# Expert windows that finish their own rows: a residual add and a scatter in each window, sorting in two steps, separate waits for high and low halves, and two whole weight parts instead of three

## The reference

```python
def _L0_ffn_ref(x, w_gate, b_gate, W1, b1, W2, b2):
    logits = x_flat @ w_gate + b_gate
    probs = jax.nn.softmax(logits, axis=-1)
    route_p = jnp.max(probs, axis=-1)
    route_idx = jnp.argmax(probs, axis=-1)
    h = jax.nn.relu(jnp.einsum('nd,edm->enm', x_flat, W1) + b1[:, None, :])
    y = jnp.einsum('enm,emd->end', h, W2) + b2[:, None, :]
    return (y[route_idx, jnp.arange(n)] * route_p[:, None]).reshape(b, t, d)
x = x + _L0_ffn_ref(_layernorm(x, axis=-1), ...)
```

## Time and profile before

| | us |
|---|---|
| time, median of 3 runs | 441.27 (439.25 to 441.68) |
| the profiled execution's own time | 440.8 |
| its span, first to last instruction | 439.1 |
| first matmul of the first window | 187.2 |
| last product of the last window done | 421.2 |
| TensorE busy | 402.3 (92%) |
| VectorE busy | 319.6 (73%) |
| ScalarE busy | 257.0 (59%) |
| GpSimd busy | 34.9 (8%) |

### The profile page before, as it was taken

The page is one execution under the profiler, slowest core; times in us unless marked ns, Lnnn a source line. Parts: engine busy times, 40 slices in busy tenths (PEclk is TensorE's granted clock), DMA queues, the critical chain, the costliest instruction groups (busy, mean ns, idle before and its releaser), DMA issues.

```text
span 439.1 us, 5615 instructions
## 1 busy us (share of the span) xinstructions
PE 402.3 (92%) x1660; PEld 280.6 (64%) x1660; DVE 319.6 (73%) x497; ACT 257.0 (59%) x388; POOL 34.9 (8%) x41
## 2 busy tenths in 40 slices
PE   5999999999999897799998999999999999999930
PEld 2855576577874356577775777767777776767710
DVE  2768767798441886579797597979889797988802
ACT  4779687773000021377686667968686796867600
POOL 2100000000000010000200202001020201002022
PEclk9799899999999997989999999999999999999995
DMA  8995382695519800100069998699898989600005
GB/s 244 414 424 184 137 294 90 223 347 195 193 48 405 312 1 6 37 15 0 0 215 355 357 406 320 199 383 368 324 355 346 351 327 373 231 1 25 1 24 191
DMA packets 33695, 95.72 MB, mean 218 GB/s; under 512 B 2690, under 2 KB 3330, under 8 KB 32132
## 3 DMA queue, kind: packets, MB, share of 16 engines
q1 hardware_dynamic: 30900, 91.61, 56.4%
q0 software_dynamic: 1136, 3.67, 2.4%
q10 hardware_dynamic: 1632, 0.11, 0.3%
HBM read 91.72 MB, written 3.67 MB: 217 GB/s over the span
## 4 chain that ended last, share of the span: by engine, by line
PE 64%; DVE 19%; issue 7%; ACT 4%; DMA 3%; POOL 1%; DVEq 0%; SPq 0%; POOLq 0%; ACTq 0%
PE bank L1463 29%; DVE w_lo L1135 12%; PE bank L1298 6%; PE bank L1279 5%; PE bank L1308 3%; DVE h_lo L1130 3%; PE bank L1232 2%; DMA ring<-in_wq_t 2%; DVE work L1122 2%; PE bank L1478 2%; PE bank L1344 2%; PE bank L1320 2%; PE bank L1287 2%; ACT ring L522 1%; PE bank L1224 1%
## 5 line engine op out<-in xcount | busy, mean ns | idle before, releaser
L1135 DVE TENSOR_TENSOR w_lo<-ring,w_hi 128x1024 fp32r<-128x1024 f32 x117 | 145.3, 1267 | 33.8 <-ACT w_hi L688 32.8
L688 ACT ACTIVATE w_hi<-ring 128x1024 fp32r<-128x1024 f32 x117 | 122.3, 1054 | 54.0 <-PE bank L1463 53.0
L1463 PE MATMUL bank<-w_hi,x_hi 128*128 128x512 f32 x144 | 49.2, 423 | 5.6 <-DVE x_lo L1149 3.2
L1463 PE MATMUL bank<-ring,work 128*128 128x512 f32 x108 | 49.9, 598 | 0.3
L1463 PE MATMUL bank<-w_hi,x_lo 128*128 128x512 f32 x144 | 45.2, 395 | 0.0
L1463 PE MATMUL bank<-w_lo,x_hi 128*128 128x512 f32 x144 | 44.9, 393 | 0.0
L1463 PEld LDWEIGHTS bank<-w_hi,x_hi 128*128 128x128 f32 x144 | 26.5, 190 | 14.6 <-issue 8.5
L1463 PE MATMUL bank<-w_hi,h_hi 128*128 128x512 f32 x90 | 33.4, 452 | 1.5 <-DVE h_lo L1130 1.5
L1203 POOL TENSOR_TENSOR small<-small,work 128x512 f32<-128x512 f32 x9 | 16.0, 1775 | 231.1 <-ACT small L694 231.1
L1463 PEld LDWEIGHTS bank<-ring,work 128*128 128x128 f32 x108 | 19.7, 189 | 20.1 <-issue 19.4
L1463 PEld LDWEIGHTS bank<-w_hi,x_lo 128*128 128x128 f32 x144 | 27.6, 192 | 6.1
(11 more groups left out here) (188 smaller groups left out, 590.3 us busy)
## 6 DMA issues: line engine op xcount, KB each, us to landing
ring<-in_w SPq DMA_DIRECT2D x32, 2048.0 KB, 10.9
ring<-in_ctx_turned SPq DMA_DIRECT2D x4, 2048.0 KB, 12.1
ring<-in_ctx SPq DMA_DIRECT2D x4, 2048.0 KB, 14.5
y_rows<-small POOLq DMA_DIRECT2D x9, 256.0 KB, 6.2
work<-in_b SPq DMA_DIRECT2D x8, 256.0 KB, 8.0
ring<-in_wq_t SPq DMA_DIRECT2D x1, 1024.0 KB, 9.2
x_sb<-in_x SPq DMA_DIRECT2D x1, 1024.0 KB, 11.7
out<-x_sb SPq DMA_DIRECT2D x4, 256.0 KB, 2.9
```

The lines of the kernel that those rows point to most:

```text
L688: act.activation(w_hi[:, n % NSPLIT, :, :], weight_part(e, n), ACT.Identity).then_inc(hi_ready, 1)
L1135: dve.tensor_tensor(w_lo[:, n % NSPLIT, :, :], weight_part(e, n), w_hi[:, n % NSPLIT, :, :], ALU.subtract).then_inc(lo_ready, 1)
L1463: ins = pe.matmul(dst, kept, moved, start=start and g == 0 and q == 0, stop=stop and g == 1 and q == len(terms) - 1)
```

## The change

1. **Whole parts.** `WHOLE` is (14, 15) instead of (6, 14, 15). Part 6 is halved: ACT makes `w_hi` of part 6 and VectorE its `w_lo` in the place where part 7's stood, and both make part 7's later, ACT behind `h_hi` for o0, VectorE behind the relu of h1.
2. **Waits apart.** TensorE waits for the high halves before the first two matmuls of a halved part, for the low rows before the next two and for `lo_ready` before the last two.
3. **Rows with their residual.** Each token's row is kept with its probability and its number (`x_ext`, 514 values). Before the windows GpSimd scatters these rows in sorted order to the scratch tensor `sorted_rows`, by four indirect DMAs. ACT's first `outputs_copy` waits for them.
4. **In each window** GpSimd loads the window's 128 rows into `x_rows_w`, once the rows of the window before have been sent; VectorE, as its last step, adds the probability times b2 to them (`bias_added`); in the next window ACT multiplies by the probability while it copies, GpSimd adds the rows, makes a small product, and scatters the result into `out` by an indirect DMA. Rows of the pad are out of bounds and dropped. The gather, the last VectorE step and SP's stores are gone.
5. **Sorting in two steps.** Batches 0 and 1 for all four banks, then batches 2 and 3. Four warming pairs instead of five stand ahead of it, and the four matmuls on zeros at the start are gone.

```diff
-WHOLE = (6, 14, 15)
+WHOLE = (14, 15)
...
-                act.activation(y_out, bank[:, Y_BANK, :], ACT.Identity).then_inc(y_copied, 1)
+                act.wait_ge(sorted_sent, 16 * NB)
+                act.wait_ge(x_rows_ready, w + 1)
+                act.activation(y_out, bank[:, Y_BANK, :], ACT.Identity, scale=x_rows_w[:, D:D + 1]).then_inc(y_copied, 1)
...
+            def bias_added(e, w):
+
+                dve.wait_ge(x_rows_loaded, 16 * w + 16)
+                dve.wait_ge(b2_loaded[e % NB2], 16 * (e // NB2 + 1))
+                dve.scalar_tensor_tensor(out=x_rows_w[:, 0:D], in0=b2_sb[e % NB2], scalar=x_rows_w[:, D:D + 1],
+                                         in1=x_rows_w[:, 0:D], op0=ALU.mult, op1=ALU.add).then_inc(x_rows_ready, 1)
...
-                        for n in (1, 2, 3, 4, 5, 7):
+                        for n in (1, 2, 3, 4, 5, 6):
                             low_part(e, w, n)
                         block_copy(w, 0)
                         block_low(w, 0)
                         block_relu(e, w, 0)
+                        low_part(e, w, 7)
...
-            for b in range(NB):
-                dve.wait_ge(gathered[b], 16)
-                dve.scalar_tensor_tensor(out=x_sb[:, b, :], in0=y_tok[:, b, :], scalar=prob[:, b:b + 1],
-                                         in1=x_sb[:, b, :], op0=ALU.mult, op1=ALU.add).then_inc(result_ready, 1)
+                        bias_added(e, w)
...
+            pool.wait_ge(rows_ready, 2)
+            pool.wait_ge(prob_ready, 1)
+            for b in range(NB):
+                pool.indirect_dma_start(sorted_rows, bass.IndirectOffsetOnAxis(ap=row_i[:, b:b + 1], axis=0),
+                                        x_ext[:, b, :], None).then_inc(sorted_sent, 16)
...
+                        pool.wait_ge(y_copied, w + 1)
+                        pool.wait_ge(rows_sent, 16 * w + 32)
+                        pool.dma_start(x_rows_w, sorted_rows[bass.ds(first_row, P), :]).then_inc(x_rows_loaded, 16)
+                        pool.wait_ge(x_rows_ready, w + 2)
                         pool.wait_ge(y_copied, w + 2)
-                        pool.tensor_tensor(y_out, y_out, b2_sb[e % NB2], ALU.add).then_inc(y_added, 1)
+                        pool.tensor_tensor(y_out, y_out, x_rows_w[:, 0:D], ALU.add).then_inc(y_added, 1)
                         pool.wait_ge(y_added, w + 2)
-                        pool.dma_start(y_rows[bass.ds(first_row, P), :], y_out).then_inc(rows_sent, 16)
+                        pool.tensor_tensor(rstd, m_half, m_half, ALU.mult)
+
+
+                        pool.indirect_dma_start(out, bass.IndirectOffsetOnAxis(ap=x_rows_w[:, D + 1:D + 2].bitcast(U32), axis=0),
+                                                y_out, None, bounds_check=NB * LQ - 1, oob_is_err=False) \
+                            .then_inc(rows_sent, 16)
...
-            pe.wait_ge(zeros_ready, 1)
-            keep_warm(4, zeros[:, 0:D])
...
-            keep_warm(5, tab[:, 0:2 * P])
...
+            keep_warm(4, tab[:, 0:2 * P])
...
+            for batches in (range(0, 2), range(2, NB)):
+                for c in range(DCH):
+                    sorting(c, batches)
...
-                        pe.wait_ge(xw_ready, w + 1)
```

92 lines of the change are left out of this document (47 added, 45 removed).

## The result

The changed kernel takes **436.16 us** (median of 4 runs, 434.83 to 437.38), the kernel before 440.6 beside it (median of 4). The ratio is 0.990, 95% interval 0.986 to 0.994. It is faster, by 4.4 us. The forecast was 430.0, with 425.5 to 437.5 as its range: the direction and the range held, but of the 11 us that the sum promised, fewer than half came. With it the time would have been 438.7, outside the range.

A forecast was written before the change was run, and what follows sets the result against it. TensorE set the pace, with small waits for VectorE's full stretch, and a serial end of 17.9 us. Terms -11.7 + 2.9 - 2.0 - 0.3 = -11.1 on 440.8 gave 429.7, forecast as 430.0, range 425.5 to 437.5.

The forecast's parts named there:

- The end, -11.7: Behind the last product: one indirect write to out replaces gather, VectorE steps and stores, ending at 427.4 instead of 439.1.
- The windows, +0.30 each: Steady windows: VectorE's longer full stretch makes each 25.80 instead of 25.50 us; +2.9 in all with small waits.
- the wait at T1: At the transposes of h1, TensorE's 0.30 wait for the copy of h1 goes, taken off its 15.03 of the cycle.
- GpSimd and the loads: In the windows: scatter, load of rows and bias_added stay hidden, by 0.5 at the slow ends.
- second rival: Windows: GpSimd holds up a w_lo in VectorE's full stretch, 0.8 a window, time 437.3; chance 0.20.
- The fourth rival: Windows: the serial loop of scatter, load of rows and bias_added sets the window, slower at 443.5; chance 0.05.
- The first, windows set by TensorE: Windows: everything of VectorE's is hidden, a window takes 24.45, time 417.7; chance 0.07.
- Into the windows, -2.0: Sorting to the first window: shorter sorting 0.5, two matmuls running ahead 0.8, clock 0.7.
- 0.7 for the clock: Start of the first window: idle stretch near 2 instead of 3.25, half of 1.6 us lost at low clock regained.
- The third rival, the late rows: Ahead of the first window: the four scatters delay ACT's first copy, +2 to +4, time 433; chance 0.10.
- The start, -0.3: Kernel start: leaving out four matmuls on zeros gives between -0.9 (clock rises sooner) and +0.3.
- case "from 425.5 to 433.5": Whole kernel: the forecast's own case, its range from the bounds of its terms; chance 0.58.

The follow-up runs named there:

- a_place: The changed kernel with the array of rows defined last, behind all other arrays; 434.19 us, ratio 0.991 to the kernel before.
- a_two: The changed kernel with TensorE reading only the first window bound behind sorting and one more ahead of each expert's loop; 436.45 us, ratio 0.996.
- w6_late: The changed kernel with part 6 whole, rows defined last and the four scatters held until TensorE used its first weight part; 430.46 us, one execution.
- a_again: The changed kernel, unedited, run again for a second trace; 435.68 us, ratio 0.991 to the kernel before.
- b_again: The kernel before, unedited, run again for a second trace; 441.68 us.
- b_nozero: The kernel before without the four matmuls on zeros at the start; 439.78 us against 439.86 beside it, ratio 1.008.
- b_shift: The kernel before with twelve matmuls on zeros at the start in place of four; 438.71 us, ratio 1.002.
- a_copy: The changed kernel with the copy of h3 made by ScalarE in place of VectorE; 430.1 us, ratio 0.975 to the kernel before.

## Why the prediction was right and wrong

**The end, -11.7: -10.3.** Right in kind, 1.4 too much. The steps up to the issue took 2.94 against 2.7. The mis-sized term is what follows: I took 3.5 from issue to the end, and 4.7 passed. The landing itself was quick, 2.25 after the issue, but this scatter moves few rows, where the forecast had 128 in mind; a landing of 3.5 would have been 1.25 worse. Then 2.4 us still lie between it and the end of the span, of which GpSimd's DRAIN is 2.04. The sum stopped at the landing and had nothing for this step, which had been hidden before (0.42 from the last landing to the end).

**The windows, +0.30 each: +0.75.** The mechanism was right and is the most certain result: the cycle through VectorE's stretch sets the window, the stretch took 10.87 where 10.94 was worked out, the waits at T1 and ahead of o2's first matmul are gone, and TensorE stands at the third matmul, for 0.94 where 1.35 was forecast. What failed is TensorE's part of the cycle, from o2's third matmul to the start of the relu of h1, for which the sum had 14.73. It took 369.42 - 26.25 = 343.17 to 358.49, thus 15.32, 0.59 more:
- 0.30 is the wait at T1 that the sum took off. It lay behind T1, ahead of TensorE's next matmul, and the relu of h1 doesn't wait for that matmul: it began 0.66 after the start of T1 before (353.14 to 353.80) and 0.64 after it now (357.85 to 358.49). So this wait was never on the cycle, and its going gave the cycle nothing. Without taking it off the sum would have come to 26.10. This is read from the two traces alone.
- 0.18 is the pace of the matmuls, by `a_place`.
- 0.11 is the first pair behind the wait, 0.57 where the same pair took 0.46 before (338.76 to 339.22). The wait moved to this pair, and the sum kept the old length for it.

15.32 + 10.87 + 0.06 (369.36 to 369.42) is 26.25. Over nine windows the 0.45 that was not forecast is 4.0 us, the largest miss of all.

**Against it, -2.6 that no term of mine had**: the stall of the third window. I took a steady window and multiplied by nine, and did not look whether all nine were alike; one of them lasted 28.06. The term for the windows came out at 8 x 0.75 - 2.56 = +3.4 and one 0.75 in the first window. So the stall hides over half of the miss of the windows: this is luck.

**GpSimd and the loads: hidden, as forecast.** The scatter lands late, though: its issue takes 1.82 and not 1.04, and the load is issued 363.64 - 354.06 = 9.6 after it, where I had 7.7. `bias_added` never held TensorE up. The *second rival* had its mechanism right, but not its place: the add takes 1.69, the small product 1.06 (0.20 at the quiet end), both beside VectorE's work ahead of T1, where the `w_lo` that begins under the add, at 351.91, takes 1.94; those of the full stretch follow each other by 1.17. The fourth rival didn't occur. The first, windows set by TensorE, is what the kernels with part 6 whole turned out to be.

**Into the windows, -2.0: about +1.8.** This step failed. What I expected to begin at `x_hi` began 1.7 later, since TensorE doesn't only wait there: it reads nine bounds, a step that the sum put at nothing. Before, the reads ended at 185.50 and `x_lo` at 186.96, so they were hidden; now they end at 187.35, behind `x_hi`, and the scatters have made them longer. `a_two` and `w6_late` show it from both sides. I had costed the scatters only by who waits for their data. The shorter idle stretch on which 0.7 for the clock rested didn't come, either: it was 3.7 instead of 3.25. That the clock rose 2.3 us later behind the first product, +1.1, is of this execution: the pair of `a_again` and `b_again` has it the other way round. The third rival, the late rows, came in part: ScalarE waited 1.63. TensorE was late already, and no wait of its own follows from it. Sorting did get shorter from the first one-hot to the last matmul, 8.35 instead of 9.44; but in executions of the kernel before this piece varies between 8.4 and 9.5 as well, so I can't credit the change with it. And 1.4 of the 1.8 lies ahead of the first one-hot, where the two kernels are alike: the clock fell earlier in that execution (at 167.4, against 170.4), and in `a_again` it did not (171.4).

**The start, -0.3: +0.8,** read at a product of TensorE behind the long stretch of the convolution (130.12 before, 130.90 after). The matmuls on zeros were indeed worth nothing (`b_nozero`). But the first real product began at 12.64, and at 11.25 to 11.78 in the other changed kernels, against 10.57 to 11.08 in those with the old rows (`b_shift`, which pushes it back itself, aside): about 0.6 later. I hadn't costed what wider rows do to the loads of the start; the first weights landed 10.8 after their issue instead of 9.2. Why, wasn't tried, and at 130 us nothing sure is left of it: the kernels with the old rows get there at 128.7 to 130.4, those with the new ones at 128.2 to 131.0.

In sum: the end 1.4 short, the windows 1.3, the way into them 3.8, the start 1.1 and the last product 0.1, together 7.7; 11.1 - 7.7 = 3.4 is what the two spans show. Of these 7.7, the 1.4 ahead of the first one-hot, the 1.1 of the clock and most of the start are what executions differ by; the windows, the end and the late first product belong to the change. The chance of 0.58 for a case "from 425.5 to 433.5" was too high, since its bounds took each term by itself from rows of before, while two of them (nine reads beside scatters, wider rows in the loads) had no row there at all.

## What to carry to other kernels

Where one engine's full stretch closes the cycle of a loop, an added step costs its full time in each turn even if it relieves the busiest engine: halving part 6 gave TensorE 0.43 a window, by the forecast's working, and cost 10 us. Find the cycle first, then test it by taking one step out of it (`a_copy`). And count a wait as part of the cycle only if the next step of the cycle comes behind it: the 0.30 at T1 did not. When waits are put apart or a release comes earlier, ask what the waiting engine still has to do for itself (reads of registers, branches), which the old wait hid. And look at each turn of a loop, not at one: the odd turn was worth 2.6 us here.
